# Longer lags in the expert loop of a routed FFN: gate and up two rounds behind, gated rows four, second products five

## The reference

```python
y   = einsum('bct,bcd->bdt', x, cond_weights[itok])      # (32, 32, 256)
xt  = y.reshape(1024, 256)
probs = softmax(xt @ w_router); top_w, top_i = top_k(probs, 4); top_w /= sum(top_w)
g   = silu(xt @ we1[e]) * (xt @ we3[e])                  # 16 experts, hidden 128
moe = sum over the 4 chosen e of top_w[e] * (g[e] @ we2[e])
shared = (silu(xt @ ws1) * (xt @ ws3)) @ ws2             # hidden 512
out = x + shared / 5 + moe * 4 / 5
```

## Time and profile before

| | us |
|---|---|
| runs: lowest, median, highest | 149.14, 149.97, 151.33 |
| profiled execution: span | 167.7 |
| TensorE matmul busy, weight load busy | 139.6, 116.3 |
| VectorE, ScalarE, GpSimd busy | 101.4, 67.7, 66.7 |
| turn of pair 0 to turn of pair 23 | 44.3 to 128.5 |
| last scatter issued | 142.9 |

### The profile page before, as it was taken

How to read it: one execution, slowest core, us unless ns; L and a number is a source line. 1 busy time by engine, 2 the same in 40 slices (tenths; PEclk the granted TensorE clock), 3 DMA queues, 4 the chain that set the end, 5 groups by cost and what they waited for, 6 DMA issues and landing times.

```text
span 167.7 us, 2807 instructions
## 1 busy us (share of the span) xinstructions
PE 139.6 (83%) x816; PEld 116.3 (69%) x816; DVE 101.4 (60%) x271; ACT 67.7 (40%) x158; POOL 66.7 (40%) x79
## 2 busy tenths in 40 slices
PE   6949999898789299989979388978989499996840
PEld 2419988686578189979969377967978378884730
DVE  1304699989299365577974487473746263116993
ACT  3004379992453333263332442285333221249200
POOL 0600000027747473654847174644737467200000
PEclk9999999999999969999999999999999999999997
DMA  1724889989354635666656333533522212299433
GB/s 32 253 63 126 262 263 335 296 286 335 110 178 131 190 125 158 207 201 192 190 170 220 146 125 127 189 119 132 199 86 96 94 63 98 81 373 418 195 121 125
DMA packets 23741, 29.81 MB, mean 178 GB/s; under 512 B 4112, under 2 KB 20496, under 8 KB 23600
## 3 DMA queue, kind: packets, MB, share of 16 engines
q1 hardware_dynamic: 19632, 19.86, 35.6%
q0 software_dynamic: 3120, 8.52, 15.4%
q10 hardware_dynamic: 976, 1.26, 2.3%
HBM read 17.58 MB, written 6.42 MB: 143 GB/s over the span
## 4 chain that ended last, share of the span: by engine, by line
PE 47%; DVE 14%; DMA 14%; ACT 8%; issue 7%; another core or an unknown queue 4%; POOL 3%; DVEq 1%; POOLq 1%; ACTq 0%; SPq 0%
PE up_ps L997 15%; PE down_ps L1013 11%; PE up_ps L991 6%; PE gate_ps L950 5%; PE down_ps L975 4%; DMA store_t<-y_of,token_i 3%; DMA itok_rows<-in_itok_B 2%; POOL result L451 2%; DMA raw<-result 2%; PE down_ps L854 2%; DVE acc L809 2%; ACT raw L566 2%; ACT gt L546 2%; DMA g<-in_L_cond_weights,cond_idx 2%
## 5 line engine op out<-in xcount | busy, mean ns | idle before, releaser
L444 POOL DMA_INDIRECT store_t<-y_of,token_i x32 | 32.6, 1018 | 48.3 <-DVE token_i L709 28.2
L451 POOL DMA_INDIRECT result<-store_t,back_i x32 | 31.2, 975 | 23.7 <-DVE store_t L791 16.3
L1013 PE MATMUL down_ps<-w,gt 128*128 x94 | 25.3, 391 | 11.9 <-ACT gt L546 9.7
L1013 PEld LDWEIGHTS down_ps<-w,gt 128*128 128x128 f32 x94 | 16.1, 189 | 15.6 <-issue 14.3
L791 DVE SCALAR_TENSOR_TENSOR store_t<-down_ps,valid,store_t 128x256 f32 x47 | 21.4, 456 | 8.6 <-DVE store_t L791 3.7
L997 PE MATMUL up_ps<-w_hi,x_hi 128*128 x78 | 23.7, 304 | 1.5 <-DVE x_lo L757 0.8
L762 DVE TENSOR_TENSOR g<-sil,up_ps 128x256 f32<-128x256 f32 (+1 forms) x24 | 9.9, 412 | 20.8 <-ACT sil L554 15.6
L554 ACT ACTIVATE sil<-up_ps 128x256 f32<-128x256 f32 (+1 forms) x24 | 9.2, 384 | 32.1 <-PE up_ps L997 18.4
L997 PE MATMUL up_ps<-w_hi,x_lo 128*128 x78 | 22.0, 282 | 0.0
L997 PE MATMUL up_ps<-w_lo,x_hi 128*128 x78 | 21.9, 281 | 0.0
L546 ACT ACTIVATE gt<-down_ps 128x256 f32<-128x256 f32 (+1 forms) x24 | 9.1, 379 | 22.6 <-PE down_ps L975 12.7
(11 more groups left out here) (153 smaller groups left out, 240.5 us busy)
## 6 DMA issues: line engine op xcount, KB each, us to landing
xt<-store_t SPq DMA_DIRECT2D x43, 128.0 KB
raw<-in_L_ffn_we SPq DMA_DIRECT2D x30, 128.0 KB, 3.4
w<-in_L_ffn_we SPq DMA_DIRECT2D x4, 512.0 KB
raw<-result SPq DMA_DIRECT2D x4, 512.0 KB, 5.0
w_lo<-result SPq DMA_DIRECT2D x4, 512.0 KB, 8.1
acc<-in_x SPq DMA_DIRECT2D x2, 512.0 KB, 5.7
y_of<-store_t ACTq DMA_DIRECT2D x1, 1024.0 KB, 6.0
out<-acc SPq DMA_DIRECT2D x3, 256.0 KB, 2.1
```

The source lines that it names most:

```text
L444: pool.indirect_dma_start(xs[:, j, :], None, y_of, bass.IndirectOffsetOnAxis(ap=token_i[:, j:j + 1], axis=0),).then_inc(tile_in[j % TT], 16)
L451: pool.indirect_dma_start(result, bass.IndirectOffsetOnAxis(ap=back_i[:, j:j + 1], axis=0), merged[:, j, :], None,).then_inc(result_out[j ...
L1013: last = pe.matmul(out_ps[b][:, h, :], gt[:, b, h, :], w2_of(experts[2 + h]), start=True, stop=True)
```

## The change

The lags become 0 (turn), 2 (gate and up), 4 (gated rows turned) and 5 (second product and merge), so that the loop has 29 rounds. Around that:

- x's high and low parts get three buffers instead of two (`XB`).
- The ring for x has three places as before but no tile of its own: pairs 0 to 5 use free tiles of `store_t`, pair 6 two tiles of `w_2`, the later ones three slots of `raw`, with waits on SyncE that these are free.
- TensorE's turn of pair n now waits by itself for x's parts of pair n-2. In rounds 2 to 5 the turn comes behind gate and up.
- ScalarE takes the turned x first in its round, from round 6 on; in rounds 0 to 5 last. VectorE likewise.
- The gate products of steps 4 and 5 of the shared expert stand in rounds 24 and 25, the up products in rounds 26 and 27, each ahead of that round's second product. What remains behind the loop is put in another order. VectorE makes the gated rows of step 4 in the last round.

The turned x, `turned_high` and `turned_low`, and TensorE's `turn_gated`, `gate_up_pair` and `down_pair` are the old bodies made into functions, with the new buffer number.

```diff
+    UP_LAG = 2
+    TURN_LAG = 4
-    LAG = 3
+    LAG = 5
+    XB = 3
+    XT_RAW = 5
...
+        def xt_of(n):
+            if n < 2 * RING:
+                return xt_early[n % RING]
+            if n == 2 * RING:
+                return w_2[:, E:E + FRONT, :]
+            return xt_ring[(n - 1) % RING]
...
                 if n >= RING:
                     sp.wait_ge(t_turned, n - RING + 1)
+                    if n == 2 * RING:
+                        sp.wait_ge(down_done, STEPS)
+                    if n == 2 * RING + 1:
+                        sp.wait_ge(t_gate_up, PLAIN)
+                        sp.wait_ge(dve_lo, max(turn[XT_RAW + FRONT + k] for k in range(RING)) + 1)
...
+                if i >= UP_LAG + PLAIN:
+                    turned_high(i)
-                if (n := pair_at(i, LAG)) is not None:
+                if (n := pair_at(i, TURN_LAG)) is not None:
...
                     act.wait_ge(t_g_turned, n + 1)
                     act.activation(gt[:, b, 0:m, :], gt_ps[b][:, 0:m, :], ACT.Copy).then_inc(t_g_out, 1)
...
-                if (n := pair_at(i, 1)) is not None:
+                if (n := pair_at(i, UP_LAG)) is not None:
...
                     act.wait_ge(t_gate_up, n + 1)
                     act.activation(t_sil[:, b, 0:m, :], gu_ps[b][:, 0:m, 0:H], ACT.Silu).then_inc(t_silu, 1)
+                if i < UP_LAG + PLAIN:
+                    turned_high(i)
...
             for i in range(PAIRS + LAG):
+                if i >= UP_LAG + PLAIN:
+                    turned_low(i)
...
-                if (n := pair_at(i, 1)) is not None:
+                if (n := pair_at(i, UP_LAG)) is not None:
...
                     dve.wait_ge(t_silu, n + 1)
                     dve.tensor_tensor(t_gated[:, b, 0:m, :], t_sil[:, b, 0:m, :], gu_ps[b][:, 0:m, H:2 * H], ALU.mult).then_inc(t_g, 1)
+                if i < UP_LAG + PLAIN:
+                    turned_low(i)
                 if i < 2:
                     add_shared(i, STEPS // 2 * (i + 1))
                 for n in SPLIT.get(i, []):
                     low(n)
...
+                if i == PAIRS + LAG - 1:
+                    gated(STEPS)
...
                 if n < 2:
                     pe.wait_ge(silu_done, STEPS - 1 + n)
+                elif n - 2 < PLAIN:
+                    pe.wait_ge(t_x_hi, n - 1)
+                else:
+                    pe.wait_ge(t_x_lo, n - 1 - PLAIN)
...
+                first = UP_LAG <= i < UP_LAG + PLAIN
+                if (n := pair_at(i, 0)) is not None and n and not first:
                     turn_pair(n)
+                if (n := pair_at(i, TURN_LAG)) is not None:
+                    turn_gated(n)
+                if (n := pair_at(i, UP_LAG)) is not None:
+                    gate_up_pair(n)
+                if first:
+                    turn_pair(i)
+                if PAIRS <= i < PAIRS + 2:
+                    pe.wait_ge(dve_lo, UNITS + 1)
+                    gate_up(STEPS + i - PAIRS, 0)
+                elif PAIRS + 2 <= i < PAIRS + 4:
+                    gate_up(STEPS + i - PAIRS - 2, 1)
                 if (n := pair_at(i, LAG)) is not None:
-                    if n >= PAIRS - KD:
-                        pe.wait_ge(dve_lo, UNITS + 1)
-                        gate_up(STEPS, 0, [n - (PAIRS - KD)])
...
+                    down_pair(n)
```

More of the change, by code:

```diff
@@ L89, in adaln_ffn @@
         acc = sb("acc", [P, TT, D])
[L90 to L92 removed]
+        cond_i = sb("cond_i", [P, 3], I32)
+        itok_rows, quarter_i, cond_idx = (cond_i[:, k:k + 1] for k in range(3))
         early_exp = sb("early_exp", [P, 2])
@@ L812, in _ @@
             dve.wait_ge(added, 4)
-            for s in range(STEPS, LAST_STEP - 1):
+            for s in range(STEPS + 1, LAST_STEP - 1):
                 gated(s)
@@ L963, in _, with turn_gated, gate_up_pair @@
             down(3)
+            def turn_gated(n):
+                b = n % 2
+                pe.wait_ge(t_g, n + 1)
+                if n < 2:
+                    pe.wait_ge(added, 2)
+                for h in range(halves(n)):
+                    last = pe.transpose(gt_ps[b][:, h, :], t_gated[:, b, h, :], ident[:, :])
+                last.then_inc(t_g_turned, 1)
+            def gate_up_pair(n):
+                b, c = n % 2, n % XB
+                if n < PLAIN:
+                    pe.wait_ge(t_x_hi, n + 1)
+                else:
+                    pe.wait_ge(t_x_lo, n - PLAIN + 1)
+                if n == PLAIN:
+                    pe.wait_ge(dve_lo, turn[UNITS - LATE - 1] + 1)
+                for h in range(halves(n)):
+                    for u, it in LATE_ITEM.items():
+                        if 2 * n + h == it:
+                            pe.wait_ge(dve_lo, turn[u] + 1)
+                    if n < PLAIN:
+                        for k in range(KD):
+                            last = pe.matmul(gu_ps[b][:, h, :], x_f[b][:, h, k * P:(k + 1) * P], pair_of(raw, experts[h], k),
+                                             start=(k == 0), stop=(k == KD - 1))
+                        continue
+                    m = 0
+                    for k in range(KD):
+                        for a, w in [(0, w_hi), (1, w_hi), (0, w_lo)]:
+                            last = pe.matmul(gu_ps[b][:, h, :], (x_hi, x_lo)[a][:, c, h, k * P:(k + 1) * P],
+                                             pair_of(w, experts[h], k), start=(m == 0), stop=(m == 3 * KD - 1))
+                            m += 1
+                last.then_inc(t_gate_up, 1)
@@ L964, in _, with down_pair @@
+            def down_pair(n):
+                b = n % 2
+                pe.wait_ge(t_g_out, n + 1)
+                if n >= 2:
+                    pe.wait_ge(t_merged, 2 * (n - 1))
+                else:
+                    pe.wait_ge(added, 4)
+                for h in range(halves(n)):
+                    last = pe.matmul(out_ps[b][:, h, :], gt[:, b, h, :], w2_of(experts[2 + h]), start=True, stop=True)
+                last.then_inc(t_down, 1)
             for i in range(PAIRS + LAG):
-                if (n := pair_at(i, 0)) is not None and n:
+                first = UP_LAG <= i < UP_LAG + PLAIN
+                if (n := pair_at(i, 0)) is not None and n and not first:
@@ L966, in _ @@
                     turn_pair(n)
-                if i > 1:
-                    experts = load_experts(i - 1)
-                if (n := pair_at(i, LAG)) is not None:
-                    b = n % 2
-                    pe.wait_ge(t_g, n + 1)
-                    if n < 2:
-                        pe.wait_ge(added, 2)
-                    for h in range(halves(n)):
-                        last = pe.transpose(gt_ps[b][:, h, :], t_gated[:, b, h, :], ident[:, :])
-                    last.then_inc(t_g_turned, 1)
@@ L1001, in _ @@
-                if (n := pair_at(i, LAG)) is not None:
-                    b = n % 2
-                    if n >= PAIRS - KD:
-                        pe.wait_ge(dve_lo, UNITS + 1)
-                        gate_up(STEPS, 0, [n - (PAIRS - KD)])
-                    pe.wait_ge(t_g_out, n + 1)
-                    if n >= 2:
-                        pe.wait_ge(t_merged, 2 * (n - 1))
-                    else:
-                        pe.wait_ge(added, 4)
-                    for h in range(halves(n)):
-                        last = pe.matmul(out_ps[b][:, h, :], gt[:, b, h, :], w2_of(experts[2 + h]), start=True, stop=True)
-                    last.then_inc(t_down, 1)
```

91 lines of the change are left out of this document (34 added, 57 removed).

## The result

The changed kernel takes **157.56 us** (median of 4 runs, 156.53 to 158.71) against 149.69 us of the kernel before in the same rounds: a ratio of 1.049 (95% interval 1.041 to 1.057). It is slower, as forecast, but 2.6 us above the forecast of 155.0 and 0.56 us above the range.

A forecast was written before the change was run, and what follows sets the result against it. TensorE's unbroken rounds of 2.96 us were taken to bound the loop, pair 20's product the end. Start +2.5, drain +3.7 and pauses -1.1 made +5.1 on 149.97: 155.0 us, 8-in-10 range 146.5 to 157.

The forecast's parts named there:

- Slack, and the pauses: TensorE's waits for ScalarE's copy of gated rows: longer lags hide pauses up to about 3.5 us, gaining 1.1 us when timed.
- Rival A: The profile's ScalarE pauses are real in timed runs, so the change gains: 146.6 us at f = 0.55; chance 0.18 (f over 0.53).
- f: Share of the profile's 18.8 us of pauses present in a timed run; below 0.17 in the forecast, break-even at 0.36.
- Start: VectorE reaches pair 0's gated rows later, so TensorE waits 2.85 instead of 0.3 us before their turn: +2.5 us.
- Rival C: VectorE's low parts finish sooner, so the start costs nothing: 152.6 us; chance 0.27, shared with f from 0.17 to 0.53.
- The clock: TensorE's clock after the new wait at the start: no drop taken, +1.5 us kept for the range.
- rival B: TensorE's clock falls after the new pause at the start: 156.5 us; chance 0.1.
- Drain: Two gate products, a gated-rows turn and half a gate and up move ahead of pair 20's product: +3.7 us on item 40.
- Scatter and tail: After the loop: last scatter ends 8.9 us after item 40's merge, at GpSimd's pace; the tail behind is untouched.
- SyncE's ring: Copies of x: pair 7's now waits for gate and up 3, landing about when needed; cost 0, bound +1 us.
- pair 7 of my sum: Pair 7's copy into the ring for x, expected at 63.1 to 64.0 against a need at 64.0.
- 18.8 us: Cost of pauses in the first profile of the kernel before, up to the merge of pair 20's first item.

The follow-up runs named there:

- Before again: The kernel before, unchanged, profiled a second time: 150.71 us (149.71 to 154.11, 8 runs), profiled span 148.4 us.
- g1: Kernel before, with only VectorE's gated rows of pair 0 put behind the second shared add and low parts 11 and 12: 152.35 us, 1.008 of before.
- the repeat: The changed kernel, word for word, run and profiled again: 156.16 us (154.70 to 157.49, 6 runs), 1.031 of before.
- e1: Changed kernel with the shared expert's gate and up products put back where the kernel before has them: 155.95 us, 1.026 of before.
- e4: Kernel before with step 4's whole gate product ahead of pair 20's second product, instead of halves in the last two rounds: 152.29 us, 1.012 of before.
- e3: Changed kernel with shared products back in their old places and pair 0's gated rows ahead of VectorE's second add and low parts 11, 12: 155.28 us, 1.027 of before.

## Why the prediction was right in sign and 2.6 us low

**Slack, and the pauses: the -1.1 us was wrong.** I set a stall-free *span* of 148.9 against the median *time* of 149.97 and took the difference for pauses. A run's time has 1.7 to 2.1 us around its span. With them the stall-free kernel runs 150.6 to 151.0 us, above the median; no pause was left to gain. The sum itself was good (148.4 measured). Rival A falls with it: the second trace of before has none of these pauses, and f is about zero, in the part to which I gave 0.55. (By its own formula f = 0.55 gives about 146.8 us, not 146.6.)

**Start: the wait is right, its price is not.** VectorE's delay is 2.55 us (2.49 forecast), TensorE's wait 1.8 (2.85 forecast), and the price while the clock stays up is 0.9. Before again shows what I lacked:

```profile
49.66 0.65 PE L950 MATMUL gate_ps<-ident,xt 128*128 128x128 f32 x4 [1.44 <-DMA xt<-store_t]
...
52.69 0.41 PE L975 MATMUL down_ps<-ident,g 128*128 128x128 f32 x2
52.94 1.89 PE L991 MATMUL up_ps<-raw,sil 128*128 x8
```

There TensorE comes to these gated rows at 52.69, 1.65 us after they were ready (50.63 + 0.41), because a copy of x was late. Of the 2.55 us these 1.65 were free: 0.9 is left, the distance of the third gate and up at 52.94 from the one at 53.85 above. g1 gives the same for this edit alone, if both are counted from the start of VectorE's seven low parts (43.92 in before again, 43.96 in the repeat, 45.45 in g1): the third gate and up begins 9.02, 9.89 and 9.90 us behind it, so 0.87 and 0.88 us later than before. (The 0.81 is g1's second piece, which counts from the first turn; the repeat's own is only 0.08 longer than before's once 3.39 are added, because its first turn is 1.0 us late.) Rival C ("the start costs nothing") was closer on this step than the forecast.

**The clock: I took no drop, and the profiled run had one.** It is 1.67 us here; my bound was +1.5 and rival B's chance 0.1. But the wait does not bring it every time. A pause of 1.57 to 1.82 us for these rows stands in four traces (changed, its repeat, e1, g1), and the clock fell behind it in one. The Trainium skill (TensorE: Matmul & The Clock Gate, HAM oscillation) says that an idle gap between bursts, if it is long enough, brings the slow clock back; these traces agree once in four. My bounds of 2.55 and 3.24 us fall too: the clock fell behind 1.82 us here and did not behind 2.55 in the first trace, so the length of the pause alone doesn't decide it. In other executions the clock falls ahead of the loop. In g1's trace it does, where before again (1.00) has the same instructions:

```profile
20.00:24.00 4.00, 4.00 (x14) 3.28 (x13) 3.17 (x21) 1.70 (x4) 0.00 (x0) 0.68 0.87 271
```

How much is chance shows in the runs themselves. g1's twelve lie in three groups: 150.7 to 151.0 us at a mean granted clock of 0.993 to 0.995, 152.3 to 152.5 at 0.975 to 0.985, 154.0 to 154.2 at 0.965. The changed kernel's ten runs: 154.7 to 155.2 at 0.978 to 0.983 (three), 156.5 to 157.8 at 0.955 to 0.974 (six), 158.7 at 0.960. In the first comparison all four of the change's runs were in the two upper groups, while the kernel before had three of four at 149.1 to 150.0; later it ranged to 154.3. The later ratio of 1.031 (only 3 runs of the change are in it) and the traces' 153.2 - 148.4 = 4.8 us (3.2%) tell the cost at an even clock better than 1.049, as far as so few runs can. Why the clock falls in one execution and not in the next stays open.

**Drain: right.** Forecast +3.7, measured 3.71 in five traces. e1 took two of its terms out (2.78 against 2.80), and e4 put one of them alone into the kernel before (1.39 against 1.40).

**Scatter and tail: right.** 7.9 us from item 40 to the last scatter's start, 8.9 to its end, the rest equal within 0.2. The last scatter is still later than the last merge. That the pace of GpSimd would bind as soon as the drain gets shorter (e1, e3) I had not seen.

**SyncE's ring: about 0.4.** The repeat waits 0.4 us for a copy into `raw`, the first trace 0.5. Not the pair 7 of my sum, but inside its bound of 1.

**Not foreseen: the first turn.** It starts 0.7 to 1.5 us later in the four traces of the change's family that have no drop ahead of the loop (43.95 to 44.59) than in before again and e4 (43.27, 43.14). GpSimd's first gather is issued at 35.5 to 35.7 in all of them; ScalarE's copies that need the gathered tiles wait longer for them. VectorE's list does not wait for this turn, so it swallows most of the delay at the start. The cause is open. One lead, not tested: the DMA engines are still 0.89 and 0.94 busy in 40 to 44 us in the two traces of the changed kernel, and 0.54 and 0.60 in before again and e4. The first trace of before has this turn at 44.30 too, with its first gather at 36.35.

Put together for an even clock: 0.9 (start, with the late first turn in it) + 3.7 (drain) + 0.2 (copies) = 4.8, from 148.4 to 153.2. On the median of the first comparison that is 154.5, and the lowest three of ten runs are 154.7 to 155.2. The forecast of 155.0 meets them, but partly by luck: 1.6 too much at the start against a gain of 1.1 that didn't exist. In the first trace of the changed kernel the 7.1 us over before again (155.5 against 148.4) are 1.0 at the start, 1.7 of clock, 0.5 of waiting for a copy, 3.7 of drain and 0.2 of rest. What the other three runs of the first comparison hold is argued from their mean clocks and not shown.

The **failed steps**, as the prediction put them: "a timed run holds about 1.1 of the 18.8 us", where there was no such pause; "I take no drop", where the traced run lost 1.67 us; and the +2.5 at the start, which took TensorE of the kernel before to wait 0.3 us there and measured 0.9, since a late copy of x had already made it 1.65 us late. With 1.67 for the clock the sum would have been 156.7; rival B, with 156.5, was nearest to the 157.56.

## What to carry to other kernels

Before a stall in one profile is made the aim of a change, profile the kernel a second time, and compare spans with spans. Longer lags remove waits only where these recur. What they added here is work ahead of the last items of the loop, and that was priced to 0.02 us by counting what stands before the item that releases the end. Where four engines run strictly in order and close to each other, moving one late thing uncovers the next: ask for each piece of work that is taken out of the way what TensorE was waiting for just before it.

## What was unexpected in the hardware

- One execution of the same program took 167.7 us with pauses of ScalarE of 2 to 4 us, another 148.4 us without any. Of the 105 timed runs of this family none took more than 159.93 us.
- A granted clock of 0.57 over 4 us after a pause of 1.8 us, and none after the same pause in three other traces.
- The twelve timed runs of one program (g1) fall into groups 1.5 to 1.7 us apart that go with the mean granted clock. A comparison of four runs with four can be off by that much.
